# Fills by a written table, four weight products as 32-column tiles, and the last token tiles by pairs

## The reference

```python
x = L0_attn_in_features                      # (1, 2048, 256)
h = layernorm(x)
Q, K, V = (h @ W.T  for W in q_proj, k_proj, v_proj)      # 16 heads of 16
attn = softmax(causal(Q @ K.T / 4)) @ V
x = x + attn @ o_proj.T
h = layernorm(x)
base = h @ W.T + b                           # (2048, 256)
logits = h @ gate_w.T + gate_b               # 8 experts, the best 2 are taken
ranks = einsum('nd,erd->ner', h, lora_A)     # 8 experts x 16 ranks
out = x + base + sum over the 2 experts of gate_e * (ranks_e @ lora_B_e.T)
```

## Time and profile before

| | |
|---|---|
| median of 3 runs | 362.51 us (360.95 to 364.44) |
| the profiled execution | 361.78 us, span 359.8 us |
| granted TensorE clock | full speed in all 40 slices |
| busy share of the span | TensorE 91%, ScalarE 76%, VectorE 57%, GpSimd 13% |

### The profile page before, as it was taken

The page is one execution under the profiler, slowest core; times in us unless marked ns, Lnnn a source line. Parts: engine busy times, 40 slices in busy tenths (PEclk is TensorE's granted clock), DMA queues, the critical chain, the costliest instruction groups (busy, mean ns, idle before and its releaser), DMA issues.

```text
span 359.8 us, 6664 instructions
## 1 busy us (share of the span) xinstructions
PE 326.0 (91%) x2486; PEld 135.8 (38%) x2486; DVE 203.5 (57%) x671; ACT 272.9 (76%) x306; POOL 46.2 (13%) x69
## 2 busy tenths in 40 slices
PE   6967969899999999999999999999999889999973
PEld 2545524454333454533333233223322233322562
DVE  5448787766767664625845466346337425531752
ACT  2345387788798878798998999999997988879210
POOL 5011100000311300001120121111111011110010
PEclk9999999999999999999999999999999999999999
DMA  7388167112720011164000000000000000000001
GB/s 211 94 217 225 36 171 192 29 38 45 187 57 7 24 29 32 32 155 107 12 21 0 3 16 16 0 2 15 16 1 3 0 16 15 2 15 16 0 3 61
DMA packets 21826, 19.10 MB, mean 53 GB/s; under 512 B 14496, under 2 KB 18848, under 8 KB 21792
## 3 DMA queue, kind: packets, MB, share of 16 engines
q1 hardware_dynamic: 21792, 18.64, 19.6%
HBM read 12.35 MB, written 6.29 MB: 52 GB/s over the span
## 4 chain that ended last, share of the span: by engine, by line
PE 63%; ACT 15%; DVE 10%; issue 8%; DMA 1%; POOL 0%; SPq 0%; ACTq 0%
PE acc L867 26%; ACT probs L983 13%; PE scores L850 12%; PE aux L712 7%; PE aux L757 5%; PE aux L738 4%; PE aux L718 2%; PE aux L768 2%; DMA wqkv_sb<-wqkv 1%; DVE parts L1123 1%; DVE turned L1183 1%; ACT qk L973 1%; PE scores L688 1%; DVE parts L1121 1%; DVE attn_t L1196 1%
## 5 line engine op out<-in xcount | busy, mean ns | idle before, releaser
L983 ACT ACTIVATE probs<-scores 128x1024 f32<-128x1024 f32 x272 | 257.0, 1033 | 33.7 <-PE scores L850 32.9
L867 PE MATMUL acc<-probs,v_aug 128*32 128x512 f32 (+3 forms) x1280 | 137.8, 535 | 1.9 <-DVE probs L1177 1.6
L850 PE MATMUL scores<-q_stack,k_stack 64*128 64x512 f16 (+3 forms) x640 | 82.7, 349 | 12.7 <-ACT probs L983 10.6
L850 PEld LDWEIGHTS scores<-q_stack,k_stack 64*128 64x128 f16 x640 | 23.6, 94 | 105.4 <-ACT probs L983 84.4
L867 PEld LDWEIGHTS acc<-probs,v_aug 128*32 128x32 f32 x1280 | 33.0, 109 | 53.8 <-issue 36.9
L1177 DVE TENSOR_TENSOR probs<-probs,mask_sb 128x512 f32<-128x512 f32 (+1 forms) x80 | 45.3, 591 | 7.8 <-ACT probs L983 7.7
L1228 DVE COPY ffn<-aux 128x392 f32<-128x392 f32 x12 | 6.8, 566 | 40.7 <-PE aux L757 40.7
L712 PE MATMUL aux<-xT,wqkv_sb 128*128 128x128 f32 x192 | 24.6, 281 | 3.6 <-ACT v_aug L977 1.8
L712 PEld LDWEIGHTS aux<-xT,wqkv_sb 128*128 128x128 f32 x192 | 22.3, 191 | 8.0 <-DVE v_aug L1132 3.1
L1490 POOL TENSOR_TENSOR exp_gap<-euler,top_gap 128x1 f32<-128x1 f32 x12 | 7.4, 614 | 99.6 <-DVE top_gap L1238 99.6
L1481 POOL TENSOR_TENSOR rstd<-ve,minus_half 128x1 f32<-128x1 f32 x12 | 7.5, 624 | 90.9 <-DVE ve L1102 90.9
(11 more groups left out here) (135 smaller groups left out, 274.5 us busy)
## 6 DMA issues: line engine op xcount, KB each, us to landing
q_stack<-q_dram SPq DMA_DIRECT2D x16, 256.0 KB, 4.0
k_stack<-k_dram SPq DMA_DIRECT2D x32, 128.0 KB, 3.9
x_sb<-x SPq DMA_DIRECT2D x3, 512.0 KB, 4.9
q_dram<-parts SPq DMA_DIRECT2D x24, 64.0 KB, 2.2
k_dram<-parts SPq DMA_DIRECT2D x12, 128.0 KB, 2.2
out<-ffn SPq DMA_DIRECT2D x12, 128.0 KB, 1.7
wqkv_sb<-wqkv SPq DMA_DIRECT2D x3, 256.0 KB, 4.9
x_sb<-x SPq DMA_DIRECT2D x2, 256.0 KB, 3.2
```

Of the source, the lines that this page charges most:

```text
L850: m = pe.matmul(scores[u % BANKS][:, j, col:col + n], k_stack[row:row + STACK, kb // TPC, 2 * i + p, kb % TPC * P:(kb % TPC + 1) * P], q_s ...
L867: m = pe.matmul(acc[32 * hp:32 * hp + 32, lo:CHUNK], v_aug[:, kb, QUAD * i + hp, :], probs[:, u % PROBS, hp % 2, col:col + CHUNK - lo], st ...
L983: act.activation(probs[:, u % PROBS], scores[u % BANKS][:], ACT.Exp, scale=EXP_SCALE).then_inc(exp_done, 1)
```

## The change

- The planner goes. `FILLS_BEHIND` is a table with one cell for each step from step 10 on; `place_pieces` reads it. The pieces are the same, the steps are others: `o 0` comes in step 12 and not 18; the q and k of tiles 12 to 15 come in steps 33, 36, 45 and 49 and not 28, 30, 32 and 34; `lora` is mostly alone in a step, where before it mostly shared one with the `o` of two tiles on.
- `project_qk`, `o`, `ffn` and `lora` go through `matmul_by_columns`: each matmul over 128 columns of weights becomes four over 32 columns, at columns 0, 32, 64 and 96. `project_v`, the transposes and the last four tiles are left as they were.
- ScalarE copies q and k out of `aux` after the last exp of the step, not after the second (the same in the steps of two units).
- SyncE issues the five loads of the later weights (`load_rest`) after the parts of tile 5 are stored, in step 1, and not after the loads of chunk 1.
- The last four tiles go by pairs: y of a pair is one bank (`aux` for the first), x comes as one product of 512 columns, the first of the two products with `wo` is issued ahead (for the first pair before the values of step 93), ranks have two banks of their own, VectorE measures both pairs before it normalises, all four transposes of y come before the ranks, all `base` products before the gates' transposes, and two DMAs store the result.

```diff
-def place_with(late):
-    ...
+FILLS_BEHIND = """
+    qk8, v8 x9, o0, qk9, y0, f0, v9 x10, qk10, v10 x11, -, qk11, v11 x12, g0, o1, r0, -, o2, y1, nq2,
...
+    g11, r11, -, -, -
+"""
...
+            def matmul_by_columns(to, weights, moving, start, stop):
+                for a in range(0, P, 32):
+                    m = pe.matmul(to[a:a + 32], weights[:, a:a + 32], moving, start=start, stop=stop,
+                                  tile_position=(0, a), skip_group_check=True)
+                return m
+
             def project_qk(g):
...
-                        m = pe.matmul(aux[:, n * P:(n + 1) * P], wqkv_sb[:, k, col:col + P], xT[:, k, :],
-                                      start=(k == 0), stop=(k == KH - 1))
+                        m = matmul_by_columns(aux[:, n * P:(n + 1) * P], wqkv_sb[:, k, col:col + P], xT[:, k, :],
+                                              start=(k == 0), stop=(k == KH - 1))
...
             def project_o(n, w, rows):
                 for k in range(KH):
-                    m = pe.matmul(w.bank[:, 0:D], rows[:, k, :], wo_sb[:, k, :],
-                                  start=(k == 0), stop=(k == KH - 1))
+                    m = matmul_by_columns(w.bank[:, 0:D], rows[:, k, :], wo_sb[:, k, :],
+                                          start=(k == 0), stop=(k == KH - 1))
...
             def ffn(n, w):
...
-                    m = pe.matmul(w.bank[:, 0:FFN], w.yT[:, k, :], wffn_sb[:, k, :],
-                                  start=(k == 0), stop=(k == KH - 1), skip_group_check=True)
+                    m = matmul_by_columns(w.bank[:, 0:FFN], w.yT[:, k, :], wffn_sb[:, k, :],
+                                          start=(k == 0), stop=(k == KH - 1))
...
             def lora(n, w):
                 pe.wait_ge(gatedT_ready, n + 1)
-                pe.matmul(w.out, w.gatedT, lora_b_sb[:], start=True, stop=True,
-                          skip_group_check=True).then_inc(out_psum, 1)
+                matmul_by_columns(w.out, w.gatedT, lora_b_sb[:], start=True, stop=True).then_inc(out_psum, 1)
...
-            def last_o(t):
-                pe.wait_ge(attn_t_ready, NQUAD // 2 * NCHUNK + t // 2)
-                for k in range(KH):
-                    m = pe.matmul(last_banks[t][:, 0:D], attn_t[:, (NCHUNK - 1) % 2, k, t * P:(t + 1) * P], wo_sb[:, k, :],
-                                  start=False, stop=(k == KH - 1), skip_group_check=True)
+            def last_start(p):
...
+                at = TILES - TPC + 2 * p
+                pe.matmul(y_banks[p], ident_sb[:], x_sb[:, at:at + 2, :], start=True, stop=False, skip_group_check=True)
+                pe.wait_ge(attn_t_ready, NQUAD // 2 * (NCHUNK - 1) + 1)
+                for t in (2 * p, 2 * p + 1):
+                    pe.matmul(y_bank(t), attn_t[:, (NCHUNK - 1) % 2, 0, t * P:(t + 1) * P], wo_sb[:, 0, :],
+                              start=False, stop=False, skip_group_check=True)
+
+
+            def last_o(p):
+                pe.wait_ge(attn_t_ready, NQUAD // 2 * NCHUNK + p)
+                for t in (2 * p, 2 * p + 1):
+                    m = pe.matmul(y_bank(t), attn_t[:, (NCHUNK - 1) % 2, 1, t * P:(t + 1) * P], wo_sb[:, 1, :],
+                                  start=False, stop=True, skip_group_check=True)
                 m.then_inc(last_y_psum, 1)
...
-                if at == 1:
+                if at == len(UNITS_OF[STEP_OF[u]]) - 1:
                     for name, n in PIECE_AT.get((STEP_OF[u], 0), ()):
                         if name == "project_qk":
                             store_qk(n)
...
                     if name == "project_qk":
                         store_parts(n)
+                        if n == TPC + 1:
+                            load_rest()
```

More of the change, by code:

```diff
@@ L131 @@
 POST_PIECES = ("o", "turn_y", "ffn", "turn_gated", "lora")
-POST_GAP = {"o": 2, "turn_y": 1, "ffn": 2, "turn_gated": 1, "lora": 1}
-LEFT = ("project_v", "o")
-RIGHT = ("turn_x", "turn_y", "turn_gated", "lora")
-SPARE_STEPS = 6
 def pieces_ahead(c):
@@ L149, in norms_of, with read_fill @@
     return [(("norm_q", c),), (("norm_k", c),)]
-UNIT_COLUMNS, STEP_COLUMNS, UNIT_SHARE, MOST_AHEAD = 512, 528, 2172, 2400
-PIECE_COLUMNS = {"project_qk": 4200, "project_v": 2090, "turn_x": 790, "o": 2090, "turn_y": 790, "ffn": 3120,
-                 "turn_gated": 400, "lora": 1056, "norm_q": 1080, "norm_k": 1080}
-NORMS_FROM = QK_STEPS - 20
-def step_columns(s):
-    values = sum(4 * (CHUNK - GROUPS[n].lo if GROUPS[n].lo != 2 * P else 2 * P) for n in GROUPS_AT.get(s, ()))
-    return STEP_COLUMNS + (UNIT_COLUMNS - UNIT_SHARE) * len(UNITS_OF[s]) + values
-def place_pieces():
-    for late in range(0, 40000, 200):
-        at = place_with(late)
-        if at is not None:
-            return at
-def place_with(late):
-    at, behind = {}, 0
+PIECE_OF = {"qk": "project_qk", "v": "project_v", "x": "turn_x", "o": "o",
+            "y": "turn_y", "f": "ffn", "g": "turn_gated", "r": "lora",
+            "nq": "norm_q", "nk": "norm_k", "n": "norms"}
+FILLS_BEHIND = """
+    qk8, v8 x9, o0, qk9, y0, f0, v9 x10, qk10, v10 x11, -, qk11, v11 x12, g0, o1, r0, -, o2, y1, nq2,
+    f1, y2, f2, g1, qk12, g2, v12 x13, qk13, r1, v13 x14, nk2, o3, -, r2, o4, y3, qk14, y4, v14 x15,
+    f3, qk15, v15, g3, f4, r3, o5, g4, nq3, nk3, y5, f5, r4, o6 g5, r5, o7, y6, f6, y7, -, f7, g6,
+    o8 r6, g7, r7, y8, f8, -, o9 g8, o10 r8, y9, f9, y10, f10, g9, o11 r9, -, y11, f11, g10, r10,
+    g11, r11, -, -, -
+"""
+def read_fill(cell):
+    pieces = []
+    for word in cell.split():
+        letters = word.rstrip("0123456789")
+        if letters != "-":
+            pieces.append((PIECE_OF[letters], int(word[len(letters):])))
+    return tuple(pieces)
+def place_pieces():
+    at = {}
     for n, fill in enumerate(pieces_ahead(0)):
@@ L240, in place_with @@
-    return at if not ahead and not norms and len(done) == TILES - TPC else None
+    for n, cell in enumerate(FILLS_BEHIND.split(",")):
+        if read_fill(cell):
+            at[FIRST_STEP[1] + n, 0] = read_fill(cell)
+    return at
 PIECE_AT = place_pieces()
@@ L814, in last_lora @@
                 for t in (2 * p, 2 * p + 1):
-                    pe.matmul(last_banks[t][:, 0:D], last_gatedT[:, t, :], lora_b_sb[:], start=False, stop=True,
-                              skip_group_check=True).then_inc(last_out_psum, 1)
+                    m = pe.matmul(y_bank(t), last_gatedT[:, t, :], lora_b_sb[:], start=False, stop=True,
+                                  skip_group_check=True)
+                m.then_inc(last_out_psum, 1)
             PRE = {"turn_x": turn_x, "project_qk": project_qk, "project_v": project_v, "norm_q": norm_q,
@@ L1459, in _ @@
                 step(s)
-            for t in range(3):
-                last_measure(t)
-            last_normalise(0)
-            last_normalise(1)
-            last_measure(3)
-            last_normalise(2)
-            last_normalise(3)
+            last_measure(0)
+            last_measure(1)
+            for t in range(TPC):
+                last_normalise(t)
             for p in range(2):
@@ L1469, in _ @@
             last_gates_of_all()
-            for t in range(TPC):
-                last_finish(t)
+            for p in range(2):
+                last_finish(p)
             dve.wait_ge(bound_step, BOUND_STEPS)
```

153 lines of the change are left out of this document (50 added, 103 removed).

## The result

The changed kernel takes 351.46 us (median of 4 runs, 348.68 to 353.34) where the kernel before takes 362.53 (4 runs, 360.95 to 364.44): ratio 0.969, 95% interval 0.959 to 0.978. It is faster, by 11 us. The forecast was 343, with 351 as the end of its range, and 351.46 lies 0.5 beyond that end. On another chip the same kernel took 349.83 against 362.64, ratio 0.964 (0.960 to 0.968; the ninth experiment), inside the range but still 7 us above the forecast.

What follows compares the result with a forecast made beforehand. TensorE was taken as the bound, with ScalarE near. 361.8 us - 17.6 (steps 10 to 93) - 0.4 (first project_qk pieces) - 1.0 (end) = 342.8, given as 343; 339 to 351 was to hold 8 in 10 and more.

Steps and rivals of the forecast that it cites:

- the prediction's own sum: Steps 10 to 93: priced pieces carried through in order, TensorE at most three units ahead; 269.6 before, 252.0 after, 17.6 less.
- the one on VectorE: Steps 10 to 93: VectorE as crowded as before after a chunk's sums (58% busy); new waits could cost another 3.0 us.
- The 3.0 that were kept: Steps 10 to 93: the sum for before falls 3.0 us short of the trace's 272.6; kept for the forecast too.
- Column tiles: Four fp32 products: 0.20 us less a fill, 0.22 a project_qk; alone 6.6 us in the steps, 0.4 at the start.
- Both rivals about the quartet (0.15 and 0.24): Four 32-column matmuls, 128 columns streamed, slower than 0.11 us: at 0.15, 350.5 us (chance 0.10); at 0.24, 368 (0.05).
- The table: Steps 10 to 93: work spread more evenly over the steps, 11.3 us less by the table alone.
- ScalarE's waits for scores: Steps 10 to 93: to fall from 27.6 us to about 12.
- The later copy: Copy of q and k behind the last exp: the 5.8 us of waits go, no cost beyond the carried sum.
- SyncE and the keys: Loads ahead of tile 6's stores cost nothing; chunk 3's keys reach step 55 with 1 to 2 us to spare.
- The end: Last four tiles by pairs: about 1 us less, bounds 3 less and 1 more.
- eaten by VectorE: Rival, steps 10 to 93: inputs from VectorE and chunk 3's keys late, another 3 + 2 us, 348 us; chance 0.18.
- the 5 set: Steps 10 to 93: the prediction is wrong if TensorE's waits for VectorE total above 5 us.

Runs made afterwards that it cites:

- the ninth experiment: The changed kernel again, unaltered, on another chip: 349.83 us, ratio 0.964 to the kernel before.
- 6: busy in two waits: Changed kernel with unread TensorE products ahead of the turn of gated tile 8 and the last tiles' first turn: 348.80 us, ratio 0.963.
- 10: third table, busy: Changed kernel with a third table (empty step behind the values of tile 8) and unread products in both ends' waits: 340.93 us, ratio 0.941.
- experiment 5: Changed kernel with ScalarE's copy of q and k behind the second exp again: 349.66 us, ratio 0.962.
- experiment 3: Changed kernel with two gaps in the table: empty step ahead of `o` 0, turn of gated tile 8 a step later: 349.54 us, ratio 0.965.
- 7: Changed kernel with another table, searched anew by the prediction's prices, mostly three or more steps from `ffn` to its gates: 347.42 us, ratio 0.958.
- Experiment 12: Third table and unread products at both ends, as in experiment 10, but the four products over the whole array: 347.59 us, ratio 0.958.
- 8: Experiment 7's table in the changed kernel, plus unread TensorE products in the waits at both ends: 345.00 us, ratio 0.952.
- 11: Experiment 10's kernel with ScalarE's copy of q and k behind the second exp again: 342.63 us, ratio 0.945.
- 2: Changed kernel with the four products over the whole array again; table, copy and end kept: 354.35 us, ratio 0.978.
- 4: Changed kernel with the last four tiles tile by tile, as in the kernel before: 353.31 us, ratio 0.976.

## Why the prediction was right or wrong

Faster by more than 1% was right; the size was not. By the prediction's own sum, beside the profiled execution of the changed kernel and the two versions that take its causes away:

| us | before | forecast | after | 6: busy in two waits | 10: third table, busy |
|---|---|---|---|---|---|
| up to step 10 | 59.2 | 58.8 | 61.0 | 59.6 | 58.5 |
| steps 10 to 93 | 272.6 | 255.0 | 263.1 | 259.9 | 255.0 |
| the rest of the span | 28.0 | 27.0 | 27.0 | 25.2 | 25.3 |
| span | 359.8 | 340.8 | 351.1 | 344.7 | 338.9 |

- **The step that failed** is the one on VectorE: "After a new chunk's sums VectorE is as crowded as before ..., so I keep those 3.0 ... new ones of the same kind ... could cost as much again". They did, and more: 3.9 us over the sum of the steps, 1.6 in step 12 and 2.3 in step 76. The places had been named (`o` 0 where project_qk 9 waited, `ffn` 8 and its gates two steps apart) and put aside on a mean load of 58%. The 3.0 that were kept were there too, as 0.3 to 0.8 over the sum in the steps 14, 19, 34, 50 and 51; only in 50 and 51 do waits for VectorE show (0.6 and 0.8), and in 14, 34 and 50 the earlier copy of experiment 5 took 0.4 to 0.6 away. Moving pieces in the table took the two long waits away: both in experiment 3, that of step 76 in 7, and in 10 that of step 12 as well.
- **What no term priced** is the clock. A full clock in the earlier trace rows was taken as given. In the profiled execution its falls cost about 1.7 in step 12 and 1.6 behind step 76, some 1.8 in the end (27.0 against the 25.2 of experiment 6), and in the first stretch up to 2.5 for two (61.0 against 58.5): an estimated 7.6 of the 10.3 us between the forecast's span and the measured one. With the 3.9 of waits that makes 11.5. Without the falls the end would be 1.8 and the first stretch 0.3 better than forecast, and 0.9 in the steps stays unexplained: 11.5 - 1.8 - 0.3 + 0.9 = 10.3.
- **Column tiles**: right. 6.6 forecast, 6.2 measured alone and 6.7 on the third table. A quartet of 128 columns costs 0.11: 64 pairs of weight load and matmul in 1.77 us, 28 ns a pair. Both rivals about the quartet (0.15 and 0.24) fell. The Trainium skill ("TensorE: Matmul & The Clock Gate", Back-to-back issue gap) gives about 81 ns for a matmul of 128 columns in a stream of such pairs; the trace doesn't agree, with 28 ns a pair for these column tiles of 32.
- **The table**: its evenness was right. Experiment 12 has a table without the two long waits and no column tiles, and its steps take 261.5 us, 11.1 less than before, where the forecast had 11.3 for the changed kernel's table alone. TensorE's waits for ScalarE fell by 7.6 us. ScalarE's waits for scores fell to 24.1 and not to 12, and much of the difference is TensorE's new waits and slow stretches passed on: in experiment 10, without them, they are 15.5.
- **The later copy** at nothing beyond the sum: nearly. It is worth 1.7 where the sum has 2.8.
- **SyncE and the keys**: right. Chunk 3's first keys are issued by 200.06 in the trace and the scores of step 55 start at 207.65 without a wait for them; with the 3.7 to 3.9 to landing that leaves 4 us, more than the 1 to 2 forecast, since the waits had moved step 55 back.
- **The end**: -1.0 forecast and -1.0 measured, which is luck: two errors cancel. With TensorE busy in its wait the end takes 25.2 to 25.6 us (experiments 6, 8, 10, 11, 12), so the pairs are worth 2.4 to 2.8, near the bound given. Measuring both pairs before normalising leaves a wait of 1.79 us, though, and with the fall behind it the end takes 26.2 to 27.4 in six profiles (after, 2, 3, 5, 7, 9).
- **The rival** "eaten by VectorE" had the mechanism, at 5 us and a chance of 0.18, and its mark was reached: TensorE's waits for VectorE in the steps are 5.1 us in the changed kernel, above the 5 set. The clock was in no rival, and a range that ended at 351 had no room for both.

## What to carry to other kernels

When pieces are moved closer together, price each piece's inputs on the engine that makes them, in that engine's order at that place: a mean load of 58% says nothing about a copy that stands behind a division. Then ask of every wait over a microsecond in a dense TensorE stream what the clock does behind it, in more than one profile: that of before shows full speed for its own waits, and in one execution only. Where a wait can't be moved, a few products that nothing reads kept the clock up here (experiments 6, 8 and 10 to 12), and cost nothing that could be measured. Products of 128 columns of weights in fp32 that stand between column tiles of 32 are cheaper as column tiles themselves, 0.2 us a fill.

## What was not expected of the hardware

- **The clock fell behind waits of 1.8 and 2.2 us every time, behind shorter ones rarely.** Behind the wait of 2.18 (or 2.1) us in step 76 it fell in each of the five profiles that have it (after, 2, 4, 5, 9), behind the 1.79 of the end by pairs in each of the six that have it and no added products (after, 2, 3, 5, 7, 9), and behind the one of step 12 in two (after 1.5, and 2 with 1.3 us) and not in six others (4 to 9, with 1.1 to 1.5). The waits of 1.3 to 1.5 us near 46 us have no fall in any of the fourteen profiles, the wait of 1.6 near 53 us has one in the changed kernel's first profile alone. What decides it for these shorter waits is open. With added products in the wait there was none in step 76 (6) or in the end's wait (6, 8, 10, 11, 12). One more fall stands in the last 3.2 us of the span in every profile but that of experiment 12, the kernel before too. In such a stretch the rows are about 1.8 times as long (3.37 and 1.92, 1.88 and 1.07 above; the scores in it 1.46 where they take 0.82), and it cost 1.7 us in step 12 and 1.6 behind step 76. The Trainium skill ("TensorE: Matmul & The Clock Gate", Part 1: The HAM clock gate) has two levels of the clock, and activity that lifts it to the upper; the windows' 0.50 and 1.00 agree.
- **Runs of one kernel differ by it.** The changed kernel's runs go from 347.8 us at a mean clock of 0.988 to 353.3 at 0.974; four of the six runs of experiment 10 are within 0.4 us of one another at 0.999. All 18 runs of the experiments 10 to 12 have 0.993 or more, all 10 of the changed kernel 0.989 or less. The kernel before isn't free of falls either: on the chip of experiments 5 to 8 its runs go from 361.26 us at 0.999 to 364.66 at 0.986.
- **Open:** at the start, around 22 us, the profiles of all seven versions with column tiles and no products added there fell (the changed kernel in both of its profiles), after waits of 1.2 and 0.7 to 1.3 us, and those of the two with whole products and like waits (before, with 1.2 and 1.5, and 2, with 1.2 and 0.8) did not. Whether the short column tiles have a part in that one wasn't tried apart from the waits.
